# A graph attention stage on one core: the rank of the routing a slot later, transposes and projections behind the attention product, elu's exponential a slot sooner, converted masks spread over more slots

## The reference

```
xn = layernorm(x[b]);  h = xn @ W                        # 1024 x 128
e[i,j]  = leaky_relu(f1[i] + f2[j], 0.2) where adj > 0, else -9e15
att     = softmax(e, axis over i)                        # for each column j
x[b]    = x[b] + elu(att @ h)
logits  = layernorm(x[b]) * gamma + beta, times Wr, plus br   # 1024 x 8
top 2 of the 8 logits of each node, their softmax weights
```

## Time and profile before

| | us |
|---|---|
| median of 3 runs | 1204.9 |
| the three runs | 1195.46, 1204.9, 1207.43 |
| the profiled execution, its own time | 1210.15 |
| its span (first to last instruction) | 1208.4 |
| busy in the span: PE | 1129.4 (93%) |
| ACT | 751.4 (62%) |
| DVE | 668.8 (55%) |
| POOL | 415.6 (34%) |
| mean granted TensorE clock, share of full | 0.961 |

### The profile page before, as it was taken

One profiled execution on the slowest core, in us unless ns is written; L12 is line 12 of the kernel. 1 busy time (PEld: TensorE's weight loads), 2 busy tenths in 40 slices (PEclk: granted clock), 3 DMA queues, 4 the chain that ended last, 5 costly groups with the idle time before them and its releaser, 6 DMA issues. The chain is left out here.

```text
span 1208.4 us, 17544 instructions
## 1 busy us (share of the span) xinstructions
PE 1129.4 (93%) x5321; PEld 676.5 (56%) x5353; DVE 668.8 (55%) x2146; ACT 751.4 (62%) x1090; POOL 415.6 (34%) x486
## 2 busy tenths in 40 slices
PE   2999898999889999789999999998999999999998
PEld 2455454454356777557777777776444444444443
DVE  4668887888645435356677767643343232323325
ACT  3687777788555555356766776665565656565661
POOL 5325777776678041434455445201000000000000
PEclk9598998899889999989999999999999999999999
DMA  8876567664036565322222222210000000000001
GB/s 259 324 262 237 193 229 271 248 217 193 33 104 220 166 201 174 126 66 81 77 83 81 78 77 83 58 53 1 1 0 10 9 17 9 18 9 17 9 9 36
DMA packets 69136, 130.99 MB, mean 108 GB/s; under 512 B 9918, under 2 KB 30764, under 8 KB 68012
## 3 DMA queue, kind: packets, MB, share of 16 engines
q1 hardware_dynamic: 60268, 111.96, 27.8%
q0 software_dynamic: 8192, 16.79, 4.5%
q10 hardware_dynamic: 576, 1.05, 0.2%
HBM read 77.60 MB, written 52.17 MB: 107 GB/s over the span
## 5 line engine op out<-in xcount | busy, mean ns | idle before, releaser
L2028 DVE CUSTOM_DVE_ANT_0 f_Y<-f_T,f_R 128x1024 f32<-128x1024 f32 x64 | 78.3, 1223 | 121.9 <-ACT f_R L1985 121.9
L678 PE MATMUL O<-Y,HS 128*128 128x512 f32 x256 | 144.5, 687 | 0.0
L505 POOL DMA_INDIRECT sorted_x<-V,AT_I x128 | 125.6, 981 | 54.2 <-issue 30.4
L2208 PE MATMUL eU<-XTN,V 128*128 128x512 f32 x256 | 133.5, 604 | 6.2 <-PEq L2142 6.2
L2224 PE MATMUL eY<-dGW,Vo 128*128 128x512 f32 x256 | 130.3, 596 | 1.6 <-DVE dGW L2415 1.5
L1867 POOL DMA_INDIRECT W<-sorted_y,ROW_I x96 | 91.5, 953 | 115.3 <-PE f_T L1928 97.2
L2216 PE MATMUL eU<-H,V 128*128 128x512 f32 x256 | 130.9, 593 | 0.0
L2315 ACT ACTIVATE H<-eU,bn 128x512 f32<-128x512 f32 x128 | 99.6, 778 | 39.3 <-PE eU L2208 32.2
L1948 PEld LDWEIGHTS f_O<-f_XN,f_PT 128*128 128x128 f32 x896 | 108.2, 192 | 17.8 <-issue 16.4
L1922 PE MATMUL f_T<-f_XT,f_XTA 128*128 128x512 f32 x224 | 114.6, 593 | 2.3 <-DVE f_XTA L2097 0.8
L1999 ACT COPY f_PT<-f_TP 128x512 f32<-128x512 f32 x128 | 68.8, 589 | 74.7 <-PE f_TP L1938 74.7
(11 more groups left out here) (303 smaller groups left out, 2017.5 us busy)
## 6 DMA issues: line engine op xcount, KB each, us to landing
XTN<-in_adj SPq DMA_DIRECT2D x64, 512.0 KB, 4.6
masks<-NMW SPq DMA_DIRECT2D x8, 2048.0 KB
f_MK<-masks SPq DMA_DIRECT2D x60, 256.0 KB, 2.7
sorted_y<-zero SPq DMA_DIRECT2D x39, 256.0 KB, 10.2
NMW<-sorted_x SPq DMA_DIRECT2D x39, 256.0 KB, 2.7
sorted_y<-NMW SPq DMA_DIRECT2D x39, 256.0 KB, 2.1
X<-in_x SPq DMA_DIRECT2D x8, 512.0 KB, 7.6
out_x<-X SPq DMA_DIRECT2D x16, 256.0 KB, 2.3
```

The costliest lines, as they stand in the source:

```text
L505: g_.indirect_dma_start(sorted_x, bass.IndirectOffsetOnAxis(ap=AT_I[b % 2][:, kt:kt + 1], axis=0), XR[b % 2][:, t * P:(t + 1) * P], None). ...
L678: pe.matmul(O[:, h * HALF:(h + 1) * HALF], HS[:, g % 3, :], Y[:, g % 4, h * HALF:(h + 1) * HALF], start=False, stop=(c == NT - 1)).then_in ...
L2028: v.tensor_tensor_reduce(Y[:, g % 3, :], T[g % 2][:, :], R4[:, g % 2, :], -SLOPE, 3.0e38, ALU.add, ALU.min, LOW[:, g % RING:g % RING + 1]) ...
L2208: pe.matmul(U1[j % 2][:, :], V1[:, e * P:(e + 1) * P], XTN[:, b * N + q * HALF:b * N + (q + 1) * HALF], start=True, stop=True).then_inc(u1 ...
```

## The change

- PE: `rank(b-2)` goes from the end of slot c = 0 (after `attend`) to c = 1, after `logits` and before `attend`. `turn_x` (c = 1) and `project` 0 and 1 (c = 2) go from before `attend` to behind it.
- DVE: the two instructions of `seat` that read M[0] become `seat_rows`, which runs at the very start of c = 1, before `shift`; the rest of `seat` goes from c = 0 to c = 1, after `share`. `stats(b+2)` goes from c = 1 to c = 0 (not in batch 0). The eight `convert` were in c = 0, 2, 2, 2, 3, 3, 5, 6 and are now in c = 1, 2, 2, 3, 3, 4, 5, 6.
- ACT: `grown` goes from the start of c = 3 to c = 2, after `prob` and before `copy_h`.
- POOL: the sends of a batch start one slot later (c = 2 of batch b+2 instead of c = 1) and end one slot later; after the last slot 4 sends of batch 5 are left instead of 2.
- In batch 7 the three steps of the table of full blocks go one slot later each on PE and DVE, and `turn_el(6)` waits for the table.

```diff
@@ POOL
-                    sending = b - 2 - (c == 0)
+                    sending = b - 2 - (c <= 1)
                     if sending >= 0:
                         pool.wait_ge(t_ready, g + 1)
-                        k = (c - 1) % NT
+                        k = (c - 2) % NT
                         send(sending, (2 * k, 2 * k + 1))
...
-                send(LAST - 2, (2 * NT - 2, 2 * NT - 1))
+                send(LAST - 2, range(2 * NT - 4, 2 * NT))
@@ PE, turn_el
+                    if b == LAST - 1:
+                        pe.wait_ge(table_step, TAKEN)
@@ PE, the loop
                     logits(g)
-                    if c == 1 and b < LAST:
-                        for h in range(2):
-                            turn_x(b + 1, h)
-                    if c == 2 and b < LAST:
-                        for k in range(2):
-                            project(b + 1, k)
+                    if c == 1 and b >= 2:
+                        pe.wait_ge(before_ready, 1)
+                        rank(b - 2)
...
                     if g >= 3:
                         attend(g - 3)
-                    if c == 0 and b >= 2:
-                        pe.wait_ge(before_ready, 1)
-                        rank(b - 2)
-                    if b == LAST and c == 1:
+                    if c == 1 and b < LAST:
+                        for h in range(2):
+                            turn_x(b + 1, h)
+                    if c == 2 and b < LAST:
+                        for k in range(2):
+                            project(b + 1, k)
+                    if b == LAST and c == 2:
                         pe.wait_ge(table_step, 1)
...
-                    if b == LAST and c == 2:
+                    if b == LAST and c == 3:
                         pe.wait_ge(table_step, 3)
@@ ACT
-                    if c == 3 and b >= 1:
-                        grown(b - 1)
                     relu(g)
                     if g >= 1:
                         prob(g - 1)
+                    if c == 2 and b >= 1:
+                        grown(b - 1)
@@ DVE
+                def seat_rows(b):
+                    dve.wait_ge(rk_ps, b + 1)
+                    RK = M[0]
+                    v.tensor_tensor(SEAT[:, :, :], RK[:, 0:NT * E].rearrange("p (t e) -> p t e", e=E),
+                                    NEXT[:, :].unsqueeze(1).to_broadcast([P, NT, E]), ALU.add).then_inc(seat_step, 1)
+                    dve.wait_ge(seat_step, b + 1)
+                    v.tensor_tensor(NEXT[:, :], NEXT[:, :], RK[:, NT * E:(NT + 1) * E], ALU.add).then_inc(rk_read, 1)
...
                     b, c = g // NT, g % NT
+                    if c == 1 and b >= 2:
+                        seat_rows(b - 2)
                     if c == 3 and b >= 1:
                         elu(b - 1)
                     shift(g)
                     if g >= 1:
                         share(g - 1)
-                    if c == 0 and b >= 2:
+                    if c == (b == 0) and b + 2 < B:
+                        if b == 0:
+                            dve.wait_ge(x_rest, 16 * (B - 2))
+                        stats(b + 2)
+                    if c == 1 and b >= 2:
                         seat(b - 2)
                         if b == LAST:
                             full_blocks()
-                    if c == 1 and b + 2 < B:
-                        if b == 0:
-                            dve.wait_ge(x_rest, 16 * (B - 2))
-                        stats(b + 2)
-                    if b == LAST and c == 1:
+                    if b == LAST and c == 2:
                         take_full()
-                    if b == LAST and c == 2:
+                    if b == LAST and c == 3:
                         list_full()
...
-                        for t in ((0,), (), (1, 2, 3), (4, 5), (), (6,), (7,), ())[c]:
+                        for t in ((), (0,), (1, 2), (3, 4), (5,), (6,), (7,), ())[c]:
                             convert(b + 1, t)
```

More of the change, by code:

```diff
@@ L328, in program @@
                 "largest_step", "pcol_step", "var_ready", "half_ready"))
+            seat_step = sem("b_seat_step")
             LAST, G = B - 1, B * NT
@@ L1088, in choose_second @@
                     v.tensor_tensor(dd[:, :], m2[:, :], m1[:, :], ALU.subtract).then_inc(dd_ready, 1)
+                def seat_rows(b):
[5 more added lines that the diff above has]
+                    v.tensor_tensor(NEXT[:, :], NEXT[:, :], RK[:, NT * E:(NT + 1) * E], ALU.add).then_inc(rk_read, 1)
                 def seat(b):
                     q = b % 2
-                    dve.wait_ge(rk_ps, b + 1)
-                    RK = M[0]
-                    op(v.tensor_tensor, SEAT[:, :, :], RK[:, 0:NT * E].rearrange("p (t e) -> p t e", e=E),
-                       NEXT[:, :].unsqueeze(1).to_broadcast([P, NT, E]), ALU.add)
-                    v.tensor_tensor(NEXT[:, :], NEXT[:, :], RK[:, NT * E:(NT + 1) * E], ALU.add).then_inc(rk_read, 1)
                     dve.wait_ge(rk_read, b + 1)
@@ L1275, in _ @@
                 share(G - 1)
+                seat_rows(LAST - 1)
                 seat(LAST - 1)
@@ L1372, in _ @@
                     if k == 3:
+                        seat_rows(LAST)
                         seat(LAST)
```

## The result

| | before | changed |
|---|---|---|
| median, us (20 runs each) | 1202.41 | 1211.57 |
| range of the runs | 1194.36 to 1217.22 | 1201.47 to 1216.87 |
| profiled execution, own time (span) | 1210.15 (1208.4) | 1211.37 (1209.6) |
| mean granted clock there | 0.961 | 0.960 |

The ratio is 1.0081, 95% interval 1.0059 to 1.0103: 0.8% slower, some 10 us, and inside the forecast's "within 1%", though its upper bound is beyond it. (The ratio is of the fast runs alone, so it isn't quite the 1.0076 of the two medians.) The forecast was 1207, in a range of 1190 to 1219. The two profiled executions differ by 1.2 us only, the medians by 9.2. That gap is the main thing to explain.

The account below looks back on a forecast made before the run. TensorE was busy 93% of the span, so its waits and half-clock time were taken to count. Terms of 1.7 + 0 - 2.4 - 1.0 + 1.0 + 2.5 = +1.8 us on the three-run median 1204.9 gave 1207 us, range 1190 to 1219.

Parts of the forecast that it names:

- The rank's wait turns into one for NEXT: Batches 2 to 5, c = 1: PE's waits of 1.27 (CH) and 0.36 us (NEXT) become 0.5 and 2.2.
- The structure of batches 2 to 5, +1.7: Work and waits without clock: each round of the slot loop gets 0.4 us longer, +1.7 us for four batches.
- The clock there, 0: Batches 2 to 5: one fall to half clock in each, as long as before, so 0 us; bounds -13.9 and +6.6.
- Batch 1, -2.4: `attend` covers PE's 1.47 us wait for XNT, its clock fall goes, ACT gives back 0.8: -2.4 us.
- Batch 6, -1.0: No `stats` here, so no wait for NEXT; the rank's and elu's waits shrink: -1.0 us, bounds -1.6 and 0.
- Batch 7, +1.0: Later table steps bring waits of about 1.0 and 2 us and a likelier, longer clock fall: +1.0 us, bounds -1.2 and +2.6.
- Two more sends, +2.5: POOL, ahead of the first block: two more sends at 1.26 us each, for which PE stands: +2.5 us.
- A: Rival: the clock holds in batches 2 to 5 and all 13.9 us come back, 1193 us; chance 0.14.
- B: Rival: DVE isn't late, NEXT comes in time, batches fall to DVE's floor of about 33 us, 1188 us; chance 0.10.
- C: Rival: batches 2 to 5 pay the wait for NEXT in full, with longer clock falls, 1220 us; chance 0.18.
- D: Rival: the rank's wait reappears as waits for NEXT, the forecast's mildest form, 1204 to 1207 us; chance 0.58 together with the forecast.

Follow-up runs that it names:

- all fillers: Changed kernel with sends in their old slots and products nothing reads ahead of PE's longer waits, cut to fit: 1192.14 us, 0.9924 of the kernel before.
- fitted filler: Changed kernel with two products nothing reads (four in batch 3) ahead of PE's wait for NEXT in batches 2 to 5: 1198.64 us, 0.9967 of before.

## Why the prediction was right, and which term was off

- *The rank's wait turns into one for NEXT.* Right, to a tenth: NEXT ended at +4.45 (forecast +4.6), PE came there at +2.35 (+2.4), the wait was 2.25 (2.2) in batches 4 and 5, CH 0.42 (0.5), and `shift(8b+2)` started at +8.03 (+8.3). Missed was batch 3, where the wait was 4.00. The kernel before had 2.11 there instead of 0.36, behind `batch_norms` on DVE at the end of batch 2, and I priced all four batches alike.
- *The structure of batches 2 to 5, +1.7.* Lost clock taken off, 148.02 at 0.95 is 140.6 and 154.33 at 0.91 was 140.4: +0.2, give or take 1 by the rounding of the clock, and within the bounds. (The term itself is four times 0.4, so 1.6.) DVE's list sets PE's wait for elu, as argued; the run with `stats` back shows how tightly, with 3.5 us of waiting for elu at once.
- *The clock there, 0.* In the profiles -6.5 (7.4 lost instead of 13.9), with two falls in four batches. "A wait of 2.2 is longer than the 1.6 that was followed by a fall, so I expect one fall in each of the four" is wrong as a rule: 2.67 and 2.24 were followed by none, 0.85 by 10.2 us. The trace of the kernel before had it already: its wait of 1.20 for CH in batch 2, which ended at 106.21, was followed by half clock from 107.6 to 114.4, so a wait shorter than the 1.27 of batch 6 was enough. The rule of the Trainium skill that the prediction weighed ("TensorE: Matmul & The Clock Gate", section "HAM oscillation — how this bites in real kernels"), by which only gaps clearly longer than 1 or 2 us are dangerous, holds no better. The traces show 10.2 us at half clock behind 0.85 us, and 13.7 behind 1.6 and 1.9.
- *Batch 1, -2.4.* The wait for XNT and its fall went, but `copy_h` behind `grown` (1.28 us on ACT) brought a wait of 0.85 for H and a fall behind it: +3.0 in both profiles. In the profiles with the sends back, with batch 7 back and with all fillers the batch took 33.0 at 1.00 with a wait of 0.62, which is -1.9. So the term was right for the work, and the new wait's clock was missing. The fitted filler's profile has the wait of 0.8 and no fall (33.33 at 1.00).
- *Batch 6, -1.0.* 33.67 instead of 34.68, as forecast, with elu's wait 0.88 (forecast 0.6).
- *Batch 7, +1.0.* Measured +5.2 in the first pair. The waits were as forecast (ubf 1.6 against 1.0, elu 1.9 against 2), but the fall behind them was 13.7 us, and the bound of +2.6 was too low. Against the second profile of the kernel before (35.41) it is +2.1.
- *Two more sends, +2.5.* Counted from the start of the last rank, the first block's product starts at +11.55 (336.44) instead of +8.83 (337.15), 2.7 later. PE stood 4.96 us for it instead of 3.21, as it came there 1.0 later (5.7 was forecast, on the assumption that PE comes as early). Put back, the sends shorten the wait by 2.5.
- *Put at nothing: the rest.* the sum has no term for batch 0 and what lies ahead of it, nor for what follows the first block. There the clock made -4.3 us ahead of batch 1 and +2.8 behind 344 us.
- *Sum.* 1212.0 on the profiled execution; its own time was 1211.37, and a second one's 1211.16. The terms were off by up to 6.5 us each and cancelled, so that the sum came out is luck.
- *From there to the median.* This is the step that failed: "The median of the three runs lies 5.2 lower, at 1204.9, and the sum on it gives 1207." That carries over to the changed kernel a distance that belonged to the old one. The old one's profiles, at 0.961, were unlucky for it (0.9706 over its runs); the changed one's, at 0.960, were not (0.9619). The real median was 0.2 us above the profiled execution instead of 5.2 below. In the terms of the sum it is the clock, which was forecast at 0: over the timed runs the change loses 10.9 us more to it.

The hit is in part luck for another reason too. The forecast added 1.8 to the median of three runs, 1204.9; over 20 runs the kernel before has 1202.41. So 1207 is 4.6 us off, but the change was forecast at +1.8 and measured at +9.2, five times as much.

Of the rivals, A and B (1193 and 1188) did not come: the clock didn't hold, and DVE did stay late. (The reading against B, that DVE ran without a break from c = 4 to c = 0, doesn't hold for batch 4 of the kernel before, where its shifts of 202.41 and 209.02 waited 3.99 and 2.65 us for relu during the fall.) C took the wait for NEXT as paid in full with longer falls. Its mechanism, waits that cost more by the clock behind them than by their length, fits what the fillers showed, at about 10 us and not 13, but not at NEXT alone, and elu's wait shrank where C had it grow. D and the forecast hold for the waits, but D's 1204 to 1207 doesn't.

## What to carry to other kernels

A reorder that only moves a wait from one releaser to another is not neutral. Two short waits (1.3 and 0.4 us) became one of 2.2, the kernel lost 10.9 us more to the clock, and filling that wait with products that nobody reads gave as much back (1.1%), where filling 1.27 us in the kernel before gave nothing. That the loss sits at that wait alone isn't shown: the profiles have falls in other batches too, and a fall kept away in one batch came in another. Before moving an instruction on a full engine, see which hole it fills where it goes and which hole it leaves: `stats` in c = 0 cost a wait of 2.2, and taken back it cost one of 3.5. And a pair of profiled executions can hide a difference that twenty runs show: compare the clock of each with that of its kernel's other runs before carrying a sum from one to the other.

## What was not expected of the hardware

- The two profiled executions of the changed kernel repeat each other closely (batch 1 37.87 and 37.86, batches 2 to 5 148.02 and 148.04 us, clock 0.960 and 0.961), while the timed runs of one kernel spread over 1%, and most of the spread goes with the clock (the kernel before: 1193.94 us at 0.979, 1210.94 at 0.961).
- The length of a wait doesn't tell whether half clock follows: 0.85 us was followed by 10.2 us of it, 2.67 us by none. Nor do the same waits bring the same fall: ahead of batch 1 half clock lasted 31 us, 20 us or not at all.
- A stretch at half clock can last long while PE is busy: 13.7 us, with 12.0 busy of the 13.9 around it, and 31 us, with 30.78 busy.
- PE's busy time rises with the filler and the kernel gets faster: 137.46 instead of 134.73 us busy in batches 2 to 5, in 142.72 instead of 148.02 us.
